# A fused decoder layer: whole projection tiles on TensorE, the step size inside the decay exponent, and a copy moved from VectorE to ScalarE

## The chip, the cores and the metric

The kernel runs on one core of one Trainium2 chip. The metric is the device time of one launch in microseconds, as the median of several runs. One launch computes a whole decoder layer, for 4 sequences of 256 tokens with 256 channels each (1024 tokens).

## The reference, cut to what matters

The layer has three parts, each followed by a residual sum and a layer norm: a state-space mixer with 32 heads, an expert layer chosen by token id, and a mixture of 16 experts with two picks per token. The change touches only the mixer:

```
proj = x @ Win.T                          # per head: x (64), z (64), B (128), C (128), and dt
dt   = softplus(dt_raw + dt_bias)
xc, Bc, Cc = silu(causal_conv(x)), silu(causal_conv(B)), silu(causal_conv(C))   # 4 taps in time
decay = exp(dt * A);  dtx = dt * xc
h_t = decay_t * h_(t-1) + dtx_t outer B_t;  y_t = h_t . C_t
y = y * rsqrt(mean(y*y) + 1e-6) * silu(z);  out = y @ Wout.T
```

The kernel does not step through time. With the running sum cum of dt * A inside a sequence, y_t is the sum over s <= t of (C_t . B_s) * exp(cum_t - cum_s) * dt_s * xc_s. That is a score matrix from B and C, weighed by a decay matrix, and then multiplied by x.

## The kernel before, in words

**Tiling.** The 32 heads are taken in 16 pairs (NPAIR). The projection of a pair has 6 tiles of 128 channels (NTILE): tile 0 is x of both heads, tiles 1 to 4 are B and C of head 0 and head 1, tile 5 is z. Each tile is computed for 1024 tokens in two halves of 512; one half (`project(j)`, tile j // 2, half j % 2) fills one PSUM bank with 6 matmuls of 512 columns, a product of split float32 numbers in three terms over two blocks of 128 input channels. The halves use PSUM banks 0 to 3 in turn (`ps[:, j % 4, :]`), so a tile may start only when the tile two before it has been read out. `half_read` gives the semaphore for that.

**Software pipeline.** `steps` runs steps 0 to 17. Step n does the projection and convolution of pair n (front), the scores and half of the mixing of pair n-1 (mid), and the rest of the mixing and the norm of pair n-2 (tail). Step 0 has only the front, step 1 front and mid, steps 2 to 15 all three, step 16 mid and tail, step 17 the tail. Every engine has its own written-out order of work within a step; each executes in that order, and semaphores tie them together.

**TensorE (line 529 on).** In a step: project(0); mix(2) and mix(3) and mean_square(0) of the tail; x_to_tokens(0); project(1); x_to_tokens(1); project(2); project(3); score(0); and from then on one score after each half, with mean_square(1) after the score of j = 4 and mix(0), mix(1) after the one of j = 8. `x_to_tokens(c)` turns four 128x128 blocks of the convolved x into bank 4 + c. `score(k)` (batch k // 2, head k % 2) writes bank 4 + k % 2. It waits for two things: the silu of B and C, and `ge(pe, S["v_m"], q * UNITS + k - 1)` at line 564, that is, for VectorE's weigh(k-2), which read the same bank (for k < 2 it waits for `x_scaled`, `v_xs`, instead). `mix(p, b)` multiplies x by the weighed scores and waits for weigh(2b+1).

**ScalarE (line 857 on).** z(0) and z(1) of the pair before at the start of a step. Then `copy(j)` for j = 0 to 9, one per projected half: it reads the PSUM bank, multiplies by the last tap and writes conv. Between these copies stand, at fixed places (`work`), the silu of tile 4, the table loads, squares, exp_decay(b) (the exponential of two decay matrices), and rsqrt (a logarithm and an exponential). The four other silus close the step.

**VectorE (line 1077 on).** For each tile m the taps of the convolution add shifted multiples out of PSUM. `tap(m, i)` with s = 1 waits for the copies of the halves it covers (`S["a_copy"]`). The table `TAPS_OF` (line 33) gives 6 half-wide taps for tile 0 and 4 for the others: s = 1 whole, s = 2 whole, s = 3 on each half. The s = 3 taps release the PSUM banks. At fixed places (`between`) stand `x_scaled` (line 1080: the turned x times dt into xs), `weigh(k)` (line 1089: score times decay, in place) and `gate` (y times silu(z)).

**GpSimd (line 335 on).** Splits the next pair's weights, builds the decay exponents (`log_decay`: cum_t minus cum_s, plus a causal mask), subtracts low parts (`low_part`), and multiplies the norm in (`norm`). SyncE loads a pair's weights and cum rows two steps ahead.

The lines on which the order hangs:

```
                    if mid and 3 <= j < 3 + UNITS:
                        score(j - 3)
...
                    for k, at_ in enumerate(((1, 0), (2, 0), (2, 1), (3, 0), (3, 1), (4, 0), (4, 1), (4, 3))):
                        between[at_] = [lambda k=k: weigh(k)]
```

The second says: weigh(k) stands just before tap number i of tile m, for at_ = (m, i).

Of the kernel before, what the change touches and what calls it, by code (L numbers as in the profile page):

```python
# [19 lines left out]
P = 128  # L20
# [12 lines left out]
TAPS_OF = [[(slice(h, h + 1), s) for h in (0, 1) for s in (1, 2, 3)] if m == 0 else  # L33
           [(slice(0, 2), 1), (slice(0, 2), 2), (slice(0, 1), 3), (slice(1, 2), 3)] for m in range(NCONV)]
# [20 lines left out]
HIT = 3.0e38  # L55
LN_EPS = 1e-5
# [3 lines left out]
def build_layer(nc, xT, x, winT, wdtT, a_log, dt_bias, woutT, ids, ctxT, gateT, ebias, wsh, wgu, wdn, out):  # L60
# [4 lines left out]
    with ExitStack() as ctx:  # L65
# [17 lines left out]
        dt_tok = sb("dt_tok", [P, TB, H])  # L83
# [60 lines left out]
        def take(n):  # L144
# [32 lines left out]
                 "a_copy a_z a_silu a_decay a_sq a_ln a_rs "  # L177
                 "v_tap v_xs v_m v_yz v_y "
# [52 lines left out]
        def _(sp):  # L231
# [15 lines left out]
            sp.wait_ge(S["d_dt"], 3)  # L247
# [18 lines left out]
            sp.wait_ge(S["v_xs"], 2 * NPAIR)  # L266
# [42 lines left out]
        def _(pool):  # L309
# [65 lines left out]
            def step(n, par, split_next, mid, tail, ahead):  # L375

                if mid:
                    log_decay(n - 1, 1 - par, 2)
                if tail:
                    low_part(n - 2, 1)  # L380
                if mid:
                    log_decay(n - 1, 1 - par, 3)
                if split_next:
                    split(n + 1, 1 - par)
                if tail:
                    norm(n - 2, par, 0)
                    norm(n - 2, par, 1)
                if mid:
                    low_part(n - 1, 0)
                if ahead:  # L390
                    log_decay(n, par, 0)
                    log_decay(n, par, 1)
# [102 lines left out]
        def _(pe):  # L495
# [9 lines left out]
            def turn_dt():  # L505

                pe.wait_ge(S["d_dt"], 3)
                pe.wait_ge(S["z_const"], 10)
                for i, src in enumerate((dt_l, dt_cum)):
                    for b in range(TB):  # L510
                        mm = pe.transpose(ps[:, 4 + i, b * H:(b + 1) * H], src[:, b * P:(b + 1) * P],
                                          ident[0:H, 0:H])
                mm.then_inc(S["s_dtT"], 1)
                pe.wait_ge(S["d_dtT"], 1)
# [14 lines left out]
            def step(n, par, front, mid, tail):  # L529
# [26 lines left out]
                def score(k):  # L556
                    b, h = k // 2, k % 2
                    c0, c1 = cols[b]
                    Bm, Cm = conv[:, qp, 1 + 2 * h, :], conv[:, qp, 2 + 2 * h, :]
                    ge(pe, S["a_silu"], q * NCONV + 3 + 2 * h)  # L560
                    if k < 2:
                        ge(pe, S["v_xs"], q * 2 + k + 1)
                    else:
                        ge(pe, S["v_m"], q * UNITS + k - 1)
                    pe.matmul(ps[:, 4 + k % 2, 0:T], Bm[:, c0:c0 + P], Cm[:, c0:c0 + T], start=True, stop=True)  # L565
                    pe.matmul(ps[:, 4 + k % 2, T:SC], Bm[:, c1:c1 + P], Cm[:, c1:c1 + P], start=True, stop=True  # L566
                              ).then_inc(S["s_done"], 1)

                def mix(p, b):

                    g = b // 2
                    ge(pe, S["v_m"], p * UNITS + 2 * b + 2)
                    if b % 2 == 0:
                        ge(pe, S["v_xs"], p * 2 + 1 + g)
                        ge(pe, S["a_ln"], p * 2 - 1 + g)
                    for j, (c, t) in enumerate(((0, T), (T, SC))):
                        for h in range(2):
                            ch = slice(h * HP, (h + 1) * HP)
                            mm = pe.matmul(ps[ch, 6 + g, (b % 2) * T + j * P:(b % 2) * T + T], xs[:, 2 * b + j, ch],  # L579
                                           decay[:, 2 * b + h, c:t], start=(j == 0), stop=(j == 1),  # L580
                                           skip_group_check=True)
                            if j == 1:
                                mm.then_inc(S["y_done"], 1)
# [12 lines left out]
                for j in range(2 * NTILE):  # L596
                    if front:
                        project(j)
                    if tail and j == 0:
# [6 lines left out]
                    if mid and j < 2:  # L606
                        x_to_tokens(j)
                    if mid and 3 <= j < 3 + UNITS:
                        score(j - 3)
                    if mid and j == 8:  # L610
                        mix(q, 0)
                        mix(q, 1)
                    if tail and j == 4:
                        mean_square(r, 1)
# [218 lines left out]
        def _(act):  # L833
# [22 lines left out]

            def step(n, par, front, mid, tail):
# [13 lines left out]
                def copy(j):  # L871
                    tile, hf = j // 2, j % 2
                    ge(act, S["u_done"], n * 12 + j + 1)
                    if j == 0 and not (isinstance(n, int) and n < 2):
# [3 lines left out]
                                   scale=w_raw[:, par, tap:tap + 1]).then_inc(S["a_copy"], 1)  # L878

# [25 lines left out]
                if isinstance(n, int) and n == 0:  # L905
                    work[0] += [lambda: softplus(0)]
                    work[1] += [lambda: softplus(1), lambda: softplus(2)]
                    work[2] += [lambda: softplus(3)]
                if mid:
                    work[0] += [lambda: silu(q, qp, 4)]  # L910
                if tail:
                    work[1] += [lambda: square(r, 1)]
                if mid or tail:
                    work[1] += [lambda: act.preload_act_table_set("natural_log_exp_and_others")]
                if mid:
                    for b, j in enumerate((2, 4, 6, 8)):
                        work[j] += [lambda b=b: exp_decay(b)]
                    work[8].append(lambda: square(q, 0))
                if tail:
                    work[3] += [lambda: rsqrt(r, 0)]  # L920
                    work[6] += [lambda: rsqrt(r, 1)]
# [122 lines left out]
        def _(dve):  # L1044
# [8 lines left out]
            def sum_dt():  # L1053
# [9 lines left out]
                link(dve.tensor_tensor(dt_l, dt_l, dt_ch, ALU.add))  # L1063
                link(dve.tensor_scalar(dt_da, dt_l, head_c[:, 2:3], -1.0, ALU.mult, ALU.mult))
# [4 lines left out]

            def take_dt():  # L1070
                dve.wait_ge(S["s_dtT"], 1)
                dve.tensor_copy(dt_tok[:, :, :], ps[:, 4, 0:TB * H].rearrange("p (b h) -> p b h", b=TB))
                dve.tensor_copy(cum_tok[:, :, :], ps[:, 5, 0:TB * H].rearrange("p (b h) -> p b h", b=TB)  # L1073
# [3 lines left out]
            def step(n, par, front, mid, tail):  # L1077
                q, qp, r, rp = n - 1, 1 - par, n - 2, par

                def x_scaled(c):  # L1080

                    ge(dve, S["xt_done"], q * 2 + c + 1)
                    ge(dve, S["y_done"], q * UNITS)
                    dve.tensor_tensor(xs[:, 4 * c:4 * c + 4, :].rearrange("p b (h c) -> p b h c", h=2),  # L1084
                                      ps[:, 4 + c, :].rearrange("p (b h c) -> p b h c", b=4, h=2),
                                      dt_tok[:, 4 * c:4 * c + 4, bass.ds(q * 2, 2)].unsqueeze(3)
                                      .broadcast_to([P, 4, 2, HP]), ALU.mult).then_inc(S["v_xs"], 1)
# [34 lines left out]
                if mid:  # L1122
                    between[0, 3] = [lambda: x_scaled(0)]
                    between[0, 5] = [lambda: x_scaled(1)]
                    for k, at_ in enumerate(((1, 0), (2, 0), (2, 1), (3, 0), (3, 1), (4, 0), (4, 1), (4, 3))):
                        between[at_] = [lambda k=k: weigh(k)]
                    between[4, 2] = [lambda: gate(q, qp, 0)]
                if tail:
                    between[0, 4] = [lambda: gate(r, rp, 1)]
                if isinstance(n, int) and n == 0:  # L1130
                    between[1, 0] = [sum_dt]
                for m in range(NCONV):
                    for i in range(len(TAPS_OF[m])):
                        for f in between.get((m, i), []):
                            f()
                        if front:
                            tap(m, i)
            steps(dve, step, take_dt)
# [253 lines left out]
```

## Time and profile before

| | us |
|---|---|
| median of 3 runs (lowest, highest) | 762.57 (761.0, 764.87) |
| the profiled execution, its own time | 762.01 |
| its span, first to last instruction | 760.3 |
| TensorE busy (share of the span) | 676.9 (89%) |
| VectorE busy | 522.8 (69%) |
| ScalarE busy | 430.1 (57%) |
| GpSimd busy | 437.8 (58%) |

The mixer's steps take the first two thirds of the span; the expert parts follow and are the same in both kernels. Durations of matmuls overlap: one starts before the end of the last is recorded, so the distance between starts (the pitch) tells what one costs. The same holds on the other engines by some 0.1 us: an instruction's pitch is a little under its duration where the next one does not depend on it. In the listings, PE is TensorE, PEld its weight load, DVE VectorE, ACT ScalarE, POOL GpSimd, and Lnnn the line of the kernel.

### The profile page before, as it was taken

To read this page: it belongs to the slowest core of one execution; us is meant where nothing else is said; L and a number is where in the kernel's file an instruction comes from. 1 tells how busy PE (TensorE), PEld (TensorE's weight loads), DVE (VectorE), ACT (ScalarE), POOL (GpSimd) and SP (SyncE) were. 2 spreads that over 40 slices of the span, in tenths; PEclk is the share of its full clock that TensorE was granted. 3 is DMA by queue.
4 is the path that set the end of the run, shared out by engine and by line. 5 is a ranking of instruction groups with operands and counts; after the bars stand their busy time and mean duration, and the time that the engine had idled before them with its cause. 6 is when DMAs were issued, how large, how long until landed. Compare 5 with 4: busy or idle time off the path is not lost.

```text
span 760.3 us, 11331 instructions
## 1 busy us (share of the span) xinstructions
PE 676.9 (89%) x3376; PEld 521.3 (69%) x3376; DVE 522.8 (69%) x803; ACT 430.1 (57%) x701; POOL 437.8 (58%) x382
## 2 busy tenths in 40 slices
PE   6599999999999999999999999899999986999930
PEld 3477777777777777777777777688846864677720
DVE  5988988988989989989889889512337343222236
ACT  4366777787787687687777777721011242333321
POOL 4076887787787777878868864754000014733134
PEclk9899999999999999999999999999999998999975
DMA  3221121121111211211211200430092401333324
GB/s 141 117 87 54 56 98 42 55 86 50 57 51 61 81 42 57 95 42 55 97 42 55 97 0 0 141 110 1 1 339 75 111 21 28 93 99 99 79 72 128
DMA packets 19968, 57.41 MB, mean 76 GB/s; under 512 B 2998, under 2 KB 13110, under 8 KB 17206
## 3 DMA queue, kind: packets, MB, share of 16 engines
q1 hardware_dynamic: 17686, 50.92, 19.6%
q0 software_dynamic: 2256, 6.16, 3.3%
q8 instruction: 14, 0.23, 0.1%
q14 instruction: 12, 0.10, 0.0%
HBM read 50.78 MB, written 6.29 MB: 75 GB/s over the span
## 4 chain that ended last, share of the span: by engine, by line
PE 51%; DVE 23%; issue 12%; ACT 9%; POOL 2%; DMA 1%; DVEq 1%; ACTq 0%; SPq 0%; POOLq 0%
DVE conv L1109 18%; PE ps L551 13%; PE ps L524 7%; PE ps L579 6%; PE ps L745 5%; PE ps L671 4%; PE ps L645 4%; PE ps L785 4%; ACT conv L877 3%; DVE decay L1093 2%; POOL conv L489 2%; ACT decay L883 2%; ACT y_hi L888 1%; PE ps L763 1%; PE ps L565 1%
## 5 line engine op out<-in xcount | busy, mean ns | idle before, releaser
L1109 DVE SCALAR_TENSOR_TENSOR conv<-ps,w_raw,conv 128x506 f32<-128x506 f32 (+3 forms) x352 | 324.6, 935 | 48.2 <-ACT conv L877 44.6
L551 PE MATMUL ps<-x_hi,w_hi 128*128 128x512 f32 x384 | 166.1, 433 | 29.8 <-DVE conv L1109 27.2
L877 ACT ACTIVATE conv<-ps,w_raw 128x512 f32<-128x512 f32 x160 | 109.3, 684 | 109.4 <-PE ps L551 109.2
L551 PE MATMUL ps<-x_hi,w_lo 128*128 128x512 f32 x384 | 151.6, 395 | 0.0
L551 PE MATMUL ps<-x_lo,w_hi 128*128 128x512 f32 x384 | 151.1, 393 | 0.0
L353 POOL TENSOR_TENSOR decay<-cum_b,cum_tok 128x512 f32<-128x512 f32 (+1 forms) x128 | 103.3, 829 | 35.5 <-DVE cum_tok L1073 23.8
L551 PEld LDWEIGHTS ps<-x_hi,w_hi 128*128 128x128 f32 x384 | 72.7, 189 | 56.2 <-DVE conv L1109 41.7
L373 POOL TENSOR_TENSOR y_lo<-y_sq,y_hi 128x512 fp32r<-128x512 f32 x32 | 41.3, 1289 | 80.1 <-ACT y_sq L889 80.1
L359 POOL TENSOR_TENSOR decay<-decay,mask 128x512 f32<-128x512 f32 x64 | 82.7, 1292 | 5.0
L551 PEld LDWEIGHTS ps<-x_hi,w_lo 128*128 128x128 f32 x384 | 72.5, 189 | 16.8
L551 PEld LDWEIGHTS ps<-x_lo,w_hi 128*128 128x128 f32 x384 | 73.0, 190 | 10.1
L862 ACT ACTIVATE conv<-conv 128x1024 f32<-128x1024 f32 x80 | 79.4, 1049 | 0.2
L565 PE MATMUL ps<-conv 128*128 128x256 f32 x256 | 76.4, 380 | 2.0 <-DVE xs L1084 1.6
L1093 DVE TENSOR_TENSOR decay<-ps,decay 128x384 f32<-128x384 f32 x128 | 70.2, 549 | 7.4 <-ACT decay L883 4.9
L937 ACT ACTIVATE ln_v<-ln_m,eps_ln 128x1 f32<-128x1 f32 x24 | 7.1, 295 | 90.6 <-DVE ln_m L1159 90.6
L524 PE MATMUL ps<-late,y_all 128*128 128x256 f32 x256 | 56.7, 379 | 0.2 <-DVE xs L1148 0.2
L565 PEld LDWEIGHTS ps<-conv 128*128 128x128 f32 x256 | 47.5, 188 | 13.2 <-issue 2.5
L458 POOL DMA_INDIRECT xb<-x_scratch,y_all x31 | 30.0, 967 | 42.5 <-PE ps L721 37.5
L343 POOL TENSOR_TENSOR w_lo<-w_raw,w_hi 128x1536 fp32r<-128x1536 f32 x15 | 53.0, 3531 | 1.2
L883 ACT ACTIVATE decay<-decay 128x768 f32<-128x768 f32 x64 | 53.4, 836 | 0.0
L566 PEld LDWEIGHTS ps<-conv 128*128 128x128 f32 x256 | 48.5, 190 | 6.7
L524 PEld LDWEIGHTS ps<-late,y_all 128*128 128x128 f32 x256 | 48.2, 190 | 6.9 <-DVE xs L1148 0.6
(166 smaller groups left out, 1027.1 us busy)
## 6 DMA issues: line engine op xcount, KB each, us to landing
cum_b<-cum_scratch SPq DMA_DIRECT2D x16, 1024.0 KB, 4.7
w_raw<-in_winT SPq DMA_DIRECT2D x16, 778.0 KB, 4.4
y_all<-in_wgu SPq DMA_DIRECT2D x4, 1408.0 KB, 10.7
ys_scratch<-y_blk SPq DMA_DIRECT2D x31, 128.0 KB, 1.7
late<-in_wdn SPq DMA_DIRECT2D x2, 1408.0 KB
late<-in_woutT SPq DMA_DIRECT2D x1, 2048.0 KB, 8.2
y_all<-in_xT SPq DMA_DIRECT2D x1, 1024.0 KB, 4.9
conv<-in_x SPq DMA_DIRECT2D x1, 1024.0 KB, 5.5
```

Source lines behind the costliest of these rows:

```text
L343: pool.tensor_tensor(w_lo[:, par, :], raw, w_hi[:, par, :].bitcast(F32), ALU.subtract).then_inc(S["w_split"], 1)
L353: pool.tensor_tensor(decay[:, 2 * b:2 * b + 2, c:t], cum_b[:, qp, :, b * T + j * P:(b + 1) * T], cum_tok[:, 2 * b + j, bass.ds(q * 2, 2)]. ...
L359: pool.tensor_tensor(diag, diag, mask[:, :].unsqueeze(1).unsqueeze(1).broadcast_to([P, 2, 2, P]), ALU.add).then_inc(S["p_arg"], 1)
L524: mm = pe.matmul(ps[:, b % 2, 0:D], y_all[:, i, b * P:(b + 1) * P], wo_sb[:, i, :], start=(i == 0), stop=(i == NPAIR - 1))
L551: mm = pe.matmul(ps[:, j % 4, :], wp[:, par, w], xp[:, kk, t], start=(i == 0), stop=(i == 5))
L565: pe.matmul(ps[:, 4 + k % 2, 0:T], Bm[:, c0:c0 + P], Cm[:, c0:c0 + T], start=True, stop=True)
L566: pe.matmul(ps[:, 4 + k % 2, T:SC], Bm[:, c1:c1 + P], Cm[:, c1:c1 + P], start=True, stop=True).then_inc(S["s_done"], 1)
L862: act.activation(conv[:, pp, tile, :], conv[:, pp, tile, :], ACT.Silu).then_inc(S["a_silu"], 1)
L877: act.activation(conv[:, par, tile, hf * 512:(hf + 1) * 512], ps[:, j % 4, :], ACT.Copy, scale=w_raw[:, par, tap:tap + 1]).then_inc(S["a_c ...
L883: act.activation(d, d, ACT.Exp).then_inc(S["a_decay"], 1)
L1093: dve.tensor_tensor(decay[:, k, :], ps[:, 4 + k % 2, 0:SC], decay[:, k, :], ALU.mult).then_inc(S["v_m"], 1)
L1109: dve.scalar_tensor_tensor(out=o[:, :, s:], in0=u[:, :, 0:T - s], scalar=w_raw[:, par, c:c + 1], in1=o[:, :, s:], op0=ALU.mult, op1=ALU.ad ...
```

## The change

On TensorE the two halves of a tile are projected back to back, and everything else stands between tiles: after tile 0 the tail's mixes and mean square and both x_to_tokens, after tiles 1 to 4 two scores each (before the last two of these mix(0), mix(1)). On VectorE x_scaled is gone, tile 0 has 4 taps like the others, and the weighs and gates stand at other places. On ScalarE the turned x is copied by `take_x`, and squares and rsqrt stand at other places. dt_s is no longer multiplied into x: instead cum_s - log(dt_s) takes the place of cum_s in the decay exponent. The dt part in step 0 gains a lower clamp of dt, a logarithm and a subtraction, and the turning of dt into tokens falls away.

```diff
-TAPS_OF = [[(slice(h, h + 1), s) for h in (0, 1) for s in (1, 2, 3)] if m == 0 else
-           [(slice(0, 2), 1), (slice(0, 2), 2), (slice(0, 1), 3), (slice(1, 2), 3)] for m in range(NCONV)]
+TAPS_OF = [[(slice(0, 2), 1), (slice(0, 2), 2), (slice(0, 1), 3), (slice(1, 2), 3)] for m in range(NCONV)]
...
 GpSimd, step():
                     log_decay(n - 1, 1 - par, 2)
+                    log_decay(n - 1, 1 - par, 3)
                 if tail:
                     low_part(n - 2, 1)
-                if mid:
-                    log_decay(n - 1, 1 - par, 3)
...
 TensorE, turn_dt():
-                pe.wait_ge(S["d_dt"], 3)
+                pe.wait_ge(S["d_dt"], 5)
...
-                for i, src in enumerate((dt_l, dt_cum)):
-                    for b in range(TB):
-                        mm = pe.transpose(ps[:, 4 + i, b * H:(b + 1) * H], src[:, b * P:(b + 1) * P],
-                                          ident[0:H, 0:H])
+                for b in range(TB):
+                    mm = pe.transpose(ps[:, 4, b * H:(b + 1) * H], dt_ch[:, b * P:(b + 1) * P], ident[0:H, 0:H])
...
 TensorE, score(k):
                     if k < 2:
-                        ge(pe, S["v_xs"], q * 2 + k + 1)
+                        ge(pe, S["a_xs"], q * 2 + k + 1)
...
 TensorE, step():
-                for j in range(2 * NTILE):
+                for tile in range(NTILE):
                     if front:
-                        project(j)
-                    if tail and j == 0:
+                        project(2 * tile)
+                        project(2 * tile + 1)
+                    if tail and tile == 0:
                         mix(r, 2)
                         mix(r, 3)
                         mean_square(r, 0)
...
-                    if mid and j < 2:
-                        x_to_tokens(j)
-                    if mid and 3 <= j < 3 + UNITS:
-                        score(j - 3)
-                    if mid and j == 8:
+                    if mid and tile == 0:
+                        x_to_tokens(0)
+                        x_to_tokens(1)
+                    if mid and tile == 4:
                         mix(q, 0)
                         mix(q, 1)
-                    if tail and j == 4:
+                    if mid and 1 <= tile < 5:
+                        score(2 * tile - 2)
+                        score(2 * tile - 1)
+                    if tail and tile == 2:
                         mean_square(r, 1)
...
 ScalarE:
+            def log_dt():
+                act.wait_ge(S["d_dt"], 2)
+                act.activation(dt_ch, dt_e, ACT.Ln).then_inc(S["a_dt"], 1)
...
+                def take_x(c):
+                    ge(act, S["xt_done"], q * 2 + c + 1)
+                    ge(act, S["y_done"], q * UNITS)
+                    act.activation(xs[:, 4 * c:4 * c + 4, :], ps[:, 4 + c, :].rearrange("p (b c) -> p b c", b=4), ACT.Copy
+                                   ).then_inc(S["a_xs"], 1)
...
+                    work[4] += [log_dt]
                 if mid:
                     work[0] += [lambda: silu(q, qp, 4)]
-                if tail:
-                    work[1] += [lambda: square(r, 1)]
                 if mid or tail:
                     work[1] += [lambda: act.preload_act_table_set("natural_log_exp_and_others")]
                 if mid:
+                    work[2] += [lambda: take_x(0), lambda: take_x(1)]
+                if tail:
+                    work[3] += [lambda: square(r, 1), lambda: rsqrt(r, 0)]
+                if mid:
                     for b, j in enumerate((2, 4, 6, 8)):
                         work[j] += [lambda b=b: exp_decay(b)]
-                    work[8].append(lambda: square(q, 0))
+                    work[9].append(lambda: square(q, 0))
                 if tail:
-                    work[3] += [lambda: rsqrt(r, 0)]
-                    work[6] += [lambda: rsqrt(r, 1)]
+                    work[7] += [lambda: rsqrt(r, 1)]
...
 VectorE:
                 link(dve.tensor_tensor(dt_l, dt_l, dt_ch, ALU.add))
+                link(dve.tensor_scalar(dt_e, dt_l, DT_MIN, None, ALU.max))
...
+            def less_log_dt():
+                dve.wait_ge(S["a_dt"], 6)
+                dve.tensor_tensor(dt_ch, dt_cum, dt_ch, ALU.subtract).then_inc(S["d_dt"], 1)
...
-                dve.tensor_copy(dt_tok[:, :, :], ps[:, 4, 0:TB * H].rearrange("p (b h) -> p b h", b=TB))
...
-                def x_scaled(c):
...
-                    between[0, 3] = [lambda: x_scaled(0)]
-                    between[0, 5] = [lambda: x_scaled(1)]
-                    for k, at_ in enumerate(((1, 0), (2, 0), (2, 1), (3, 0), (3, 1), (4, 0), (4, 1), (4, 3))):
+                    for k, at_ in enumerate(((2, 0), (2, 1), (3, 0), (3, 1), (4, 0), (4, 1))):
                         between[at_] = [lambda k=k: weigh(k)]
-                    between[4, 2] = [lambda: gate(q, qp, 0)]
+                    between[4, 3] = [lambda: weigh(6)]
                 if tail:
-                    between[0, 4] = [lambda: gate(r, rp, 1)]
+                    between[1, 2] = [lambda: gate(r, rp, 1)]
                 if isinstance(n, int) and n == 0:
                     between[1, 0] = [sum_dt]
+                    between[3, 0] = [less_log_dt]
...
+                if mid:
+                    weigh(7)
+                    gate(q, qp, 0)
```

## Rows read from the trace of the kernel before

**Rows 1.** The profile page: TensorE's busy time, and its granted clock in 40 slices.
```profile
PE 676.9 (89%) x3376; PEld 521.3 (69%) x3376; DVE 522.8 (69%) x803; ACT 430.1 (57%) x701; POOL 437.8 (58%) x382
...
PEclk9899999999999999999999999999999998999975
```

**Rows 2.** Waits, 73 to 477 us: engine, line, releaser: total us, times, longest.
```profile
PEld ps L551 <- DVE conv L1109: 29.6, 41, 1.4
```

**Rows 3.** ScalarE in order: start us, us, engine, line, operation; in brackets idle before.
```profile
211.51 3.90 ACT L862 ACTIVATE conv<-conv 128x1024 f32<-128x1024 f32 x4
215.32 1.06 ACT L868 ACTIVATE z_gate<-ps 128x512 f32<-128x512 f32 x2
...
220.10 0.69 ACT L877 ACTIVATE conv<-ps,w_raw 128x512 f32<-128x512 f32 x1 [2.20 <-PE ps L551]
220.69 0.60 ACT L888 ACTIVATE y_hi<-ps 128x512 fp32r<-128x512 f32 x1
...
221.78 1.28 ACT L914 ACT_TABLE_LOAD   x1
...
223.67 0.84 ACT L883 ACTIVATE decay<-decay 128x768 f32<-128x768 f32 x1
...
224.97 0.69 ACT L894 ACTIVATE y_all<-ps,eps_rms 128x512 f32<-128x512 f32 x1
...
250.91 1.28 ACT L914 ACT_TABLE_LOAD   x1
```

**Rows 4.** TensorE's matmuls in order, in the same step; first start and count.
```profile
216.05 1.52 PE L579 MATMUL ps<-decay,xs 128*64 128x256 f32 x16
217.50 0.50 PE L588 MATMUL ps<-y_hi,mean_w 128*128 128x512 f32 x1
...
218.43 0.48 PE L551 MATMUL ps<-x_hi,w_hi 128*128 128x512 f32 x1
...
219.90 0.60 PE L536 MATMUL ps<-ident,conv 128*128 128x128 f32 x4
...
220.26 0.48 PE L551 MATMUL ps<-x_hi,w_hi 128*128 128x512 f32 x1
...
223.10 0.59 PE L565 MATMUL ps<-conv 128*128 128x256 f32 x2
...
223.68 0.47 PE L551 MATMUL ps<-x_hi,w_hi 128*128 128x512 f32 x1
...
243.62 0.50 PE L551 MATMUL ps<-x_hi,w_hi 128*128 128x512 f32 x1 [0.91 <-DVE conv L1109]
```

**Rows 5.** VectorE in order, in the same step.
```profile
220.83 0.75 DVE L1109 SCALAR_TENSOR_TENSOR conv<-ps,w_raw,conv 128x510 f32<-128x510 f32 x1 [0.93 <-ACT conv L877]
...
234.25 1.27 DVE L1109 SCALAR_TENSOR_TENSOR conv<-ps,w_raw,conv 128x1020 f32<-128x1020 f32 x1
235.44 0.55 DVE L1093 TENSOR_TENSOR decay<-ps,decay 128x384 f32<-128x384 f32 x1
235.90 2.70 DVE L1109 SCALAR_TENSOR_TENSOR conv<-ps,w_raw,conv 128x1016 f32<-128x1016 f32 x3
238.52 0.55 DVE L1093 TENSOR_TENSOR decay<-ps,decay 128x384 f32<-128x384 f32 x1
```

**Rows 6.** Groups by line, all of the span: busy us, mean ns; idle before.
```profile
L1117 DVE TENSOR_TENSOR z_gate<-ps,z_gate 128x512 f32<-128x512 f32 x32 | 22.0, 687 | 6.8 <-ACT y_sq L889 6.8
```

**Rows 7.** TensorE in step 16: the first matmuls of a score after a wait.
```profile
482.13 0.67 PE L565 MATMUL ps<-conv 128*128 128x256 f32 x2 [1.17 <-DVE xs L1084]
```

**Rows 8.** VectorE in step 0: two operations on the dt arrays.
```profile
19.74 1.21 DVE L1063 TENSOR_TENSOR y_all<-y_all 32x1024 f32<-32x1024 f32 x1 [0.63 <-ACT y_all L855]
20.99 0.74 DVE L1064 TENSOR_SCALAR y_all<-y_all,head_c 32x1024 f32<-32x1024 f32 x1
```

**Rows 9.** TensorE in step 0: the first matmul after its longest wait there.
```profile
27.65 0.79 PE L551 MATMUL ps<-x_hi,w_hi 128*128 128x512 f32 x1 [6.84 <-DVE conv L1109]
```

**Rows 10.** Two microseconds of step 0: length, then each engine's busy time (instructions), PEclk, DMA.
```profile
28.00:30.00 2.00, 2.00 (x6) 1.52 (x6) 1.96 (x3) 0.00 (x0) 0.00 (x0) 0.50 1.03 430
```

More of the change, by code:

```diff
@@ L55 @@
 HIT = 3.0e38
+DT_MIN = 1.0e-30
 LN_EPS = 1e-5
@@ L82, in build_layer @@
         cum_b = sb("cum_b", [P, 2, 2, NT])
-        dt_tok = sb("dt_tok", [P, TB, H])
         cum_tok = sb("cum_tok", [P, TB, H])
@@ L176, in build_layer @@
                  "w_split u_done p_arg p_lo s_done xt_done y_done ms_done "
-                 "a_copy a_z a_silu a_decay a_sq a_ln a_rs "
-                 "v_tap v_xs v_m v_yz v_y "
+                 "a_copy a_z a_silu a_xs a_decay a_sq a_ln a_rs "
+                 "v_tap v_m v_yz v_y "
                  "ld_wo ld_xt ld_late ld_rt ln_st "
@@ L246, in _ @@
             load_pair(1, 1)
-            sp.wait_ge(S["d_dt"], 3)
+            sp.wait_ge(S["d_dt"], 4)
             sp.dma_start(cum_dram, dt_cum).then_inc(S["st_cum"], 16)
@@ L265, in _ @@
             sp.wait_ge(S["s_done"], NPAIR * UNITS)
-            sp.wait_ge(S["v_xs"], 2 * NPAIR)
+            sp.wait_ge(S["a_xs"], 2 * NPAIR)
             sp.wait_ge(S["xt_done"], 2 * NPAIR)
@@ L573, in mix @@
                     if b % 2 == 0:
-                        ge(pe, S["v_xs"], p * 2 + 1 + g)
+                        ge(pe, S["a_xs"], p * 2 + 1 + g)
                         ge(pe, S["a_ln"], p * 2 - 1 + g)
@@ L1068, in sum_dt @@
                 link(ins)
+            def less_log_dt():
+                dve.wait_ge(S["a_dt"], 6)
+                dve.tensor_tensor(dt_ch, dt_cum, dt_ch, ALU.subtract).then_inc(S["d_dt"], 1)
             def take_dt():
                 dve.wait_ge(S["s_dtT"], 1)
-                dve.tensor_copy(dt_tok[:, :, :], ps[:, 4, 0:TB * H].rearrange("p (b h) -> p b h", b=TB))
-                dve.tensor_copy(cum_tok[:, :, :], ps[:, 5, 0:TB * H].rearrange("p (b h) -> p b h", b=TB)
+                dve.tensor_copy(cum_tok[:, :, :], ps[:, 4, 0:TB * H].rearrange("p (b h) -> p b h", b=TB)
                                 ).then_inc(S["d_dtT"], 1)
@@ L1078, in step @@
                 q, qp, r, rp = n - 1, 1 - par, n - 2, par
-                def x_scaled(c):
[L1082 to L1087, printed above, removed]
                 def weigh(k):
```

## The prediction

> **What bounds the kernel now.** I read the page first: TensorE is busy 89% of the span at nearly full clock [rows 1]. Then the waits of the steady steps 2 to 15: the projection's weight loads waited 29.6 us for VectorE's taps, at most 1.4 us at a time [rows 2], some 2.1 us in each of 14 steps. Last the engines' orders in one step. One full step takes 250.91 - 221.78 = 29.13 us, from one table load to the same one a step later [rows 3].
>
> Prices by start to start. TensorE [rows 4]: a tile of two halves back to back 2.84 (220.26 to 223.10), a lone half 1.47 (218.43 to 219.90), a score 0.58, a pair of mixes 1.45, x_to_tokens 0.36, mean square and x_to_tokens together 0.93, so the mean square 0.57. A step now: 12 x 1.47 + 8 x 0.58 + 2 x 1.55 (0.1 for the change of kind) + 2 x 0.57 + 2 x 0.36 = 27.2, and with some 2 of waits it is the 29.1. So TensorE bounds it, held up by VectorE through the PSUM banks of the projection. In the new order the sum is 6 x 2.84 + the same = 26.6; without a single wait 2.5 us could be had per step.
>
> **Lags.** A copy starts 0.20 after TensorE has gone on from the half (219.90, 220.10), and the tap 0.73 after the copy [rows 3, 4, 5]: 0.93 together. VectorE: tap s = 1 to the weigh behind it 1.19, weigh 0.46, s = 2 with both s = 3 taps 2.62 [rows 5], so 1.30, 0.66, 0.66. A weigh ends 0.55 after its start, and its waiter starts 0.05 later. The gate is 0.69 long [rows 6], 0.60 by pitch as a weigh of 0.55 has 0.46. ScalarE [rows 3]: copy 0.59, exp_decay and copy 1.30, so exp_decay 0.71, the two squares 1.09, table load 1.28, four silus 3.8, z(0) and z(1) 1.0, a logarithm or an exponential of rsqrt 0.6 to 0.7.
>
> **The part that decides: where scores wait.** score(k) waits for weigh(k-2), before and after. Before, score(3) came after the first half of tile 3, and weigh(1) before the taps of tile 2: always ready. Now score(3) comes right after tile 2, and weigh(1) stands behind tap(2,0), which needs both copies of that same tile 2. TensorE must stand still meanwhile, and tile 3 stands behind score(3) on it. The same for score(5) with weigh(3) and tap(3,0), and for score(7) with weigh(5) and tap(4,0). From the end of a tile on TensorE: 0.93 + 1.19 + 0.60 = 2.72 until the odd score may start. The even score covers 0.58; two mixes and a score (2.13) cover most in the case of score(7). What is queued behind: mean_square(1), tile 3, tile 4, tile 5, and through them the copies, that is, everything.
>
> **A full step in the new order,** tile 0 starting at 0:
> - Tile 0 to 2.84, mixes to 4.38, mean square and two x_to_tokens to 5.66, tile 1 to 8.50. Its banks wait for z(0), z(1): ScalarE finishes its silus at 1.8 and z at 2.8, in time. Then copy 0, silu of tile 4, and copy 1 at 4.2; the taps of tile 0 run from 4.9 to 8.9.
> - ScalarE takes copy 2 at 7.33, take_x(0) at 7.92, take_x(1) at 8.51, exp_decay(0) at 9.10, copy 3 at 9.81. take_x is no row of before. Nearest are the copy out of PSUM of equal size (0.59 by pitch, 0.69 long) and z (0.53 by pitch); I take the copy's 0.59, bounds 0.5 to 0.7. score(0) waits 0.14 for it; scores 0 and 1 end at 9.8. Tile 2 runs to 12.64.
> - VectorE starts tile 1 at 10.54, 1.1 later than tile 1's end allows, because two take_x and exp_decay(0) stand before copy 3. Two taps, gate(1), two taps: weigh(0) at 14.96, score(2) at 15.56. TensorE has waited since 12.64: 2.9 us. tap(2,0) at 15.42 (its copies are there at 14.8, behind squares, logarithm, exponential and exp_decay(1)), weigh(1) at 16.61, score(3) at 17.21: another 1.1.
> - A score after a wait takes longer, 0.67 for its first two matmuls against 0.59 [rows 7, 4]; I take 0.67 for it. Mean square: tile 3 starts at 18.46, ends 21.30. score(5) at 24.02 (wait 2.14), tile 4 24.69 to 27.53. Mixes, score(6) to 29.65, score(7) at 30.25 (wait 0.6), tile 5 30.92 to 33.76.
>
> VectorE ends tile 4, weigh(7) and gate(0) 7 us after tile 4's end, before the next step's mix(3) and mean square want them. GpSimd, in its new order: log_decay(2), log_decay(3), then low_part(1), ready near 13, wanted at 18; the split of weights ends near 19, wanted at the next step. So these edits cost nothing, hidden by TensorE's longer step. SyncE's loads are two steps ahead and only get more time.
>
> So 33.76 against 29.13: **+4.6 per full step,** 14 x 4.62 = +64.7. Removed from VectorE are two x_scaled (0.6 each) and the extra starts of tile 0's six half taps; from TensorE 0.6 of interrupted tiles. They are in the sum and buy nothing, as the chain runs through tap, weigh, score.
>
> **Ends.** Leaving step 15, before had no 0.91 stall of the next tile 0 [rows 4]; the new step has none to save: +0.9. Step 1 has no gate and no squares before copy 4; with VectorE about 1.0 less late, +3.6. Step 16: take_x behind silu and table load, scores in pairs: +0.8 (an estimate, bounds -0.5 and +2). Step 0: VectorE gains the clamp, 0.74, and the subtraction, 1.21, both on its path to turn_dt [rows 8], loses about 0.6 of taps and 0.3 of a copy, but starts when both halves of tile 0 are copied: +1.0, bounds 0 and 2. ScalarE's extra logarithm there lies in idle time. The experts are untouched. Sum +71.0 on the profiled execution's 762.0 (its span 760.3 and 1.7 around it; the median of the runs is 762.6): **833 us**.
>
> **A rule against the change, weighed.** Row: after a wait of 6.84 us in step 0 the clock was 0.50 of full, that is 1.2 and not 2.4 GHz, and six matmuls started in 2 us [rows 9, 10]; in the steps, with waits up to 1.4, the tenths stay at 9 [rows 1, 2]. My longest wait is 2.9. By the rows it could go either way, nearer to the short waits. The Trainium skill, "TensorE: Matmul & The Clock Gate", section "A second HAM failure mode: psum-queue depth-cycling", says that frequent short idle times between groups of matmuls that cycle through PSUM banks can make the clock fall and rise again and again. No run here shows it; by that rule the time is that of rival B, without it the sum above.
>
> **Rivals.**
> - A, VectorE is not late: score(2) never waits and only the chain tile, copy, tap, weigh, odd score is left. score(3) then starts 2.72 after tile 2's end, at 15.36 instead of 17.21: 31.9 per step, +2.8, x 14 = +39, with ends +5: 806. For it: my 1.1 of ScalarE delay rests on take_x, unseen. Against: even then tile 1's taps and gate fill the time.
> - B, the clock falls once per step in the 2.9 wait. Some eight matmuls at 0.43 instead of 0.24 cost 1.6: +22, 855. Against: tile 3 and what follows keep TensorE at work.
> - C, faster: weigh(1), weigh(3) and weigh(5) are done when their odd scores come, and TensorE runs through. Then 26.8 per step, -2.3 x 14, with +1 at the start: 731. It decides at the end of tile 2: weigh(1) must have ended within 0.5 us of it. For it: VectorE has 1.8 us less to do per step. Against: weigh(1) is ordered behind a tap of that very tile, so by the code no speed of VectorE can do it.
> - D, nothing: waits and savings cancel, as in a chain of only one late score (33.76 would have to be 29.1): 762.
>
> **Chances.** Forecast 0.78 (its own range 820 to 846, from take_x, the extra per late score, and the ends), A 0.08, B 0.08, C 0.04, D 0.02. The range from 805 to 857 takes in A and B, since both are the same mechanism at other sizes. A change of under 0.5%, some 4 us, can't be told from none in this kernel. Faster 0.04, same 0.02, slower 0.94.
>
> **What would show it.** TensorE's wait of scores for the weighs (L565 for L1093, or their shifted lines), 0 in the steps now, at some 6.5 us per step; the projection's wait for taps near 0. Table loads 33.8 apart. VectorE's waits for copies up from tiles 0 and 4 to all tiles but 2. Copy 3 right behind exp_decay(0). Wrong would be: scores that never wait (C), no wait before score(2) (A), a granted clock under 0.9 in the steps (B), or the projection still waiting for taps.

## The result and the profile after

The changed kernel takes 857.1 us (median of 4 runs, 854.6 to 859.0) against 763.7 for the kernel before: a ratio of 1.123, 95% interval 1.118 to 1.127. The forecast was 833, with a range of 805 to 857. The direction and most of the size were right; the time lies at the far end of the range, outside by 0.1 us.

The page of the changed kernel, TensorE's busy time and the granted clock in 40 slices, beside [rows 1]:

```profile
PE 712.3 (83%) x3368; PEld 542.6 (63%) x3368; DVE 499.0 (58%) x740; ACT 443.5 (52%) x734; POOL 436.9 (51%) x382
...
PEclk9899998999989999999999999898999999999985
```

Two things are to be read there. VectorE, which held TensorE up before, works 24 us less (522.8 to 499.0) and the kernel is slower all the same: its work was no longer what bounds it. And TensorE is busy 35 us longer with 8 instructions fewer: some of its matmuls run slower.

The waits of the changed kernel from 80 to 570 us (engine, line, releaser: us in total, times, longest), beside [rows 2]:

```profile
DVE conv L1117 <- ACT conv L881: 152.7, 56, 4.7
...
PEld ps L561 <- DVE decay L1101: 87.6, 56, 2.8
...
PE ps L561 <- DVE decay L1101: 73.3, 56, 2.4
```

L561 is the first matmul of a score and L1101 is weigh. The 29.6 us that the projection waited for taps [rows 2] have given way to 73 us in which scores wait for weighs: 56 times, four in each of 14 steps. VectorE now waits 152.7 us for the copies of each tile. The two engines take turns where they had overlapped.

TensorE in one full step of the changed kernel, beside [rows 4] (start, us, first form of the group; in brackets idle before):

```profile
288.81 0.39 PE L547 MATMUL ps<-x_hi,w_hi 128*128 128x512 f32 x1
...
294.43 0.47 PE L547 MATMUL ps<-x_hi,w_hi 128*128 128x512 f32 x1
...
304.11 0.70 PE L561 MATMUL ps<-conv 128*128 128x256 f32 x2 [2.41 <-DVE decay L1101]
...
305.76 1.22 PE L561 MATMUL ps<-conv 128*128 128x256 f32 x2 [0.73 <-DVE decay L1101]
...
308.06 0.63 PE L547 MATMUL ps<-x_hi,w_hi 128*128 128x512 f32 x1
...
313.86 0.70 PE L561 MATMUL ps<-conv 128*128 128x256 f32 x2 [1.91 <-DVE decay L1101]
...
320.07 0.70 PE L561 MATMUL ps<-conv 128*128 128x256 f32 x2 [0.26 <-DVE decay L1101]
```

VectorE in the same step, beside [rows 5]:

```profile
299.10 1.28 DVE L1117 SCALAR_TENSOR_TENSOR conv<-ps,w_raw,conv 128x1020 f32<-128x1020 f32 x1 [1.41 <-ACT conv L881]
...
303.51 0.55 DVE L1101 TENSOR_TENSOR decay<-ps,decay 128x384 f32<-128x384 f32 x1
303.97 1.27 DVE L1117 SCALAR_TENSOR_TENSOR conv<-ps,w_raw,conv 128x1020 f32<-128x1020 f32 x1
305.16 0.55 DVE L1101 TENSOR_TENSOR decay<-ps,decay 128x384 f32<-128x384 f32 x1
```

Tile 0 starts at 288.81 and tile 1 at 294.43, 5.62 us later (forecast 5.66). score(2) starts 15.3 us behind tile 0's start (forecast 15.56), behind the weigh of 303.51; score(3) 16.95 us behind it (forecast 17.21), behind the weigh of 305.16, which stands behind the tap of tile 2 at 303.97. From here the step is slower than forecast: the score at 305.76 takes 1.22 us for its first two matmuls and not 0.67, and the matmuls behind it 0.63 instead of 0.39. The granted clock of another step shows why (length, busy time of PE, PEld, DVE, ACT, POOL, then PEclk, DMA share, GB/s):

```profile
230.00:232.00 2.00, 0.61 (x3) 0.18 (x1) 2.00 (x4) 2.00 (x4) 2.00 (x2) 1.00 0.81 332
232.00:234.00 2.00, 0.98 (x4) 0.73 (x4) 2.00 (x3) 0.07 (x1) 1.92 (x2) 0.91 0.00 0
234.00:236.00 2.00, 1.42 (x6) 1.15 (x5) 1.97 (x4) 0.00 (x0) 2.00 (x1) 0.50 0.00 0
236.00:238.00 2.00, 2.00 (x7) 1.61 (x7) 1.70 (x3) 0.00 (x0) 1.79 (x2) 0.50 0.00 0
238.00:240.00 2.00, 2.00 (x7) 1.52 (x6) 0.00 (x0) 0.23 (x1) 0.00 (x0) 0.50 0.00 0
```

TensorE stands still from 230.6 to 233.0 us, and the clock falls to half, 1.2 GHz, at 233.6, in the middle of the next matmuls. Between 200 and 440 us this happens once in each of the seven steps, five times for 3.4 us and twice for 6.8 us, and in the kernel before not once in that stretch. A full step takes 35.28 us on average ((540.06 - 81.48) / 13, by its table loads, L923), where 33.76 was forecast and 29.13 it was [rows 3]. The 13 steps fall into two groups: nine with 3.4 us at half clock take 34.8 to 35.1 us, four with 6.8 us of it 36.1 to 36.2.

### The profile page after: what moved, and what is told of

Same layout as the page of the kernel before. It is cut to its first block, busy times and chain, and to the rows that moved or that the text cites. A ratio compares the mean times of both kernels' runs of the same rounds, so it can differ in the third digit from the quotient of the medians.

```text
span 857.3 us, 11229 instructions
## 1 busy us (share of the span) xinstructions
PE 712.3 (83%) x3368; PEld 542.6 (63%) x3368; DVE 499.0 (58%) x740; ACT 443.5 (52%) x734; POOL 436.9 (51%) x382
## 4 chain that ended last, share of the span: by engine, by line
PE 58%; DVE 15%; issue 12%; ACT 10%; POOL 2%; DMA 1%; DVEq 0%; ACTq 0%; SPq 0%; POOLq 0%
PE ps L547 20%; DVE conv L1117 8%; PE ps L520 6%; PE ps L561 5%; PE ps L744 4%; ACT conv L881 4%; DVE decay L1101 4%; PE ps L670 3%; PE ps L644 3%; PE ps L784 3%; PE ps L575 3%; ACT decay L893 2%; PE ps L562 2%; POOL conv L487 2%; PE ps L532 2%
## 5 line engine op out<-in xcount | busy, mean ns | idle before, releaser
L1117 DVE SCALAR_TENSOR_TENSOR conv<-ps,w_raw,conv 128x1020 f32<-128x1020 f32 (+1 forms) x320 | 316.7, 1007 | 169.8 <-ACT conv L881 166.2
L561 PE MATMUL ps<-conv 128*128 128x256 f32 x256 | 92.5, 445 | 82.8 <-DVE decay L1101 80.3
L547 PE MATMUL ps<-x_lo,w_hi 128*128 128x512 f32 x384 | 156.8, 408 | 0.0
L547 PE MATMUL ps<-x_hi,w_lo 128*128 128x512 f32 x384 | 155.5, 405 | 0.0
L561 PEld LDWEIGHTS ps<-conv 128*128 128x128 f32 x256 | 42.3, 201 | 108.5 <-DVE decay L1101 87.6
L547 PEld LDWEIGHTS ps<-x_hi,w_hi 128*128 128x128 f32 x384 | 77.8, 203 | 28.1 <-DVE conv L1117 10.3
L547 PEld LDWEIGHTS ps<-x_hi,w_lo 128*128 128x128 f32 x384 | 76.7, 200 | 18.0
L547 PEld LDWEIGHTS ps<-x_lo,w_hi 128*128 128x128 f32 x384 | 77.5, 202 | 15.2
L367 POOL TENSOR_TENSOR y_all<-z_gate,y_all 128x512 f32 (+1 forms) x32 | 40.9, 1279 | 82.4 <-ACT y_all L906 82.4
L1101 DVE TENSOR_TENSOR decay<-ps,decay 128x384 f32<-128x384 f32 x128 | 70.2, 549 | 5.6 <-PE ps L562 5.4
L562 PE MATMUL ps<-conv 128*128 128x128 f32 x256 | 54.4, 298 | 0.0
```

What stands on the lines that cost most here:

```text
L547: mm = pe.matmul(ps[:, j % 4, :], wp[:, par, w], xp[:, kk, t], start=(i == 0), stop=(i == 5))
L1101: dve.tensor_tensor(decay[:, k, :], ps[:, 4 + k % 2, 0:SC], decay[:, k, :], ALU.mult).then_inc(S["v_m"], 1)
L1117: dve.scalar_tensor_tensor(out=o[:, :, s:], in0=u[:, :, 0:T - s], scalar=w_raw[:, par, c:c + 1], in1=o[:, :, s:], op0=ALU.mult, op1=ALU.ad ...
```

## The experiments

Theory: (1) the odd score behind a whole tile waits for a weigh that stands behind a tap of the same tile; (2) VectorE starts tile 1 late as ScalarE has the copies of x ahead of copy(3); (3) what the sum lacks is the clock. Rivals: whole tiles as such or the copy on ScalarE cost the time; or the missing 1.5 us per step are a wait and not the clock.

| label | edit | us | ratio to before (95%) |
|---|---|---|---|
| (the change) | | 857.1 | 1.123 (1.118 to 1.127) |
| e1_pairs | weighs in pairs | 793.0 | 1.037 (1.034 to 1.041) |
| e2_filler | filler in one wait | 841.2 | 1.101 (1.097 to 1.104) |
| e3_takex_early | take_x ahead of copy(2) | 839.9 | 1.100 (1.096 to 1.104) |
| e4_old_order | old order, rest kept | 772.4 | 1.011 (1.008 to 1.015) |
| e5_x_on_dve | x copy on VectorE | 845.9 | 1.107 (1.103 to 1.111) |
| e6_pairs_early | e1 and e3 | 788.7 | 1.032 (1.029 to 1.036) |
| e7_pairs_early_gate | e6, gate later | 773.4 | 1.012 (1.010 to 1.015) |
| e8_old_takex_late | e4, take_x(1) later | 765.6 | 1.002 (1.000 to 1.005) |
| e9_lag | whole tiles, scores one tile later | 740.8 | 0.970 (0.968 to 0.973) |
| e10_filler_all | filler in all long waits | 831.1 | 1.088 (1.085 to 1.092) |

**e1_pairs: the odd weighs ahead of the tap.**

```diff
-                    for k, at_ in enumerate(((2, 0), (2, 1), (3, 0), (3, 1), (4, 0), (4, 1))):
-                        between[at_] = [lambda k=k: weigh(k)]
+                    for m in (2, 3, 4):
+                        between[m, 0] = [lambda k=2 * m - 4: weigh(k), lambda k=2 * m - 3: weigh(k)]
```

> The changed kernel with one edit: on VectorE weigh(1), weigh(3), weigh(5) stand right behind weigh(0), weigh(2), weigh(4), ahead of the s = 1 tap of the tile and not behind it. Theory (the odd score waits for a tap of the tile that TensorE has just finished): the waits before score(3), score(5), score(7) vanish, the one before score(2) stays at some 2.4 us. A full step, by the same sum as in the prediction, takes 30.1 us if the clock then stays up, 31.7 if it still falls once; changed kernel 35.3. Time 784 us, or 807 with the fall. Rival (whole tiles as such, or the copy on ScalarE, cost the time): the time stays over 840 us.

793.0 us, between the two figures. One edit of the order on VectorE, with the same instructions, gives back 64 of the 93 us. Its waits from 80 to 480 us:

```profile
PEld ps L561 <- DVE decay L1101: 41.9, 32, 2.8
PE ps L561 <- DVE decay L1101: 31.1, 13, 2.4
```

One wait of 2.4 us is left per step, the one before score(2). The clock falls in every second step only; its table loads at 384.37, 415.74 and 445.79 us give a step of 31.4 with a fall and one of 30.05 without, where 31.7 and 30.1 were expected. The rival is refuted. Not all of the 64 us is the order's own: at full clock a step of the change takes 33.4 us (e10 below) and one here 30.05, which is 47 us over 14 steps. The other 17 us or so come from the clock, which falls in seven of the 14 steps for 3.4 us, where the change has it in all 14, with 6.8 us of half clock in five of them.

**e2_filler and e10_filler_all: more work, less time.** The filler's result goes to bank 6 after its last reader and is overwritten unread.

```diff
+                    if front and tail and tile == 2:
+                        ge(pe, S["a_ln"], r * 2 + 1)
+                        for i in range(8):
+                            pe.matmul(ps[:, 6, :], w_hi[:, par, 0:P], x_hi[:, 0, 0:512], start=True, stop=True)
                     if mid and 1 <= tile < 5:
                         score(2 * tile - 2)
```

> The changed kernel with eight more 512-column matmuls (their result is overwritten unread) between tile 2 and score(2) in steps 2 to 15, in the 2.4 us that TensorE waits there. More work, no wait shorter. Theory (the idle time at scores 2 and 3 lets the clock fall to 1.2 GHz for some 4 to 6 us of each step): the granted clock of the steps goes from some 0.93 to 1.00, a full step from 35.3 to 33.7 us, the time from 857 to 835 us. Rival (the extra 1.5 us per step are not the clock's but a wait that I missed): 857 us or, since the filler takes 1.9 of 2.4 us and may delay the score, up to 862.

841.2 us: 16 us faster, and 6 us short of what was expected. The clock still fell, now in every second step (at 237, 305 and 373.5 us of the stretch 200 to 440). Between two table loads a step with a fall takes 35.0 us and one without 33.4: the same instructions in one trace, 1.6 us apart. So the second run filled the others as well: 9 matmuls before score(2), 3 between scores 2 and 3, 7 between scores 4 and 5.

> The changed kernel with more 512-column matmuls in steps 2 to 15 whose result is overwritten unread, in all its long waits: 9 ahead of score(2), 3 between score(2) and score(3), 7 between score(4) and score(5). The first filler, 8 in the first wait alone, had the clock fall in every second step still. Theory (idle time of TensorE in these waits, and not one wait alone, decides on the clock; the sum of the prediction at full clock holds): no half microsecond of the steps under full clock, a full step of 33.4 to 33.8 us, time 833 us. Rival (the clock falls for another reason, or fillers delay the scores as much as they save): 841 us or more.

831.1 us. The stretch from 80 to 480 us, first of the filled kernel, then 80 to 570 us of the changed one:

```profile
80.00:480.00 400.00, 388.91 (x2003) 300.40 (x2002) 289.85 (x360) 275.41 (x396) 272.89 (x217) 1.00 0.15 56
```

```profile
80.00:570.00 490.00, 416.71 (x2053) 322.97 (x2050) 337.11 (x417) 317.39 (x456) 307.75 (x246) 0.93 0.14 48
```

266 matmuls more (14 steps of 19) and 26 us less; a step takes 351.62 - 318.27 = 33.35 us. The scores still start where VectorE lets them, as the sum has it. In this step tile 1, score(2) and score(3) start at

```profile
319.03 0.47 PE L547 MATMUL ps<-x_hi,w_hi 128*128 128x512 f32 x1
...
328.72 0.70 PE L561 MATMUL ps<-conv 128*128 128x256 f32 x2 [0.35 <-DVE decay L1110]
...
330.37 0.70 PE L561 MATMUL ps<-conv 128*128 128x256 f32 x2
```

and score(2) comes 9.69 us and score(3) 11.34 us behind tile 1's start, where the sum had 9.90 and 11.55. So what the filler takes away is the slow clock, and that cost 26 us. The time is within 2 us of the prediction's sum, 833 us. A part of that is luck: the 14 steps are 0.37 us shorter than in the sum, 5 us together, and about 3 us are lost again outside them (in step 1, which has no filler, the clock was at half for 10.2 us of the profiled execution).

**e3_takex_early: ScalarE's part.** `work[2] += take_x(0), take_x(1)` becomes `work[1] += ...`, behind the table load.

> The changed kernel with both take_x on ScalarE ahead of copy(2), after the table load, where ScalarE idles, and not behind copy(2). Theory (VectorE starts tile 1 late by 1.1 us since the copies of x stand before copy(3)): copy(3) and score(2) come 1.1 us earlier per step, time 857 - 15 = 842 us; if the shorter wait also keeps the clock up, 1.5 us more per step, 820 us. Rival (VectorE isn't late through ScalarE): 857 us, within 3.

839.9 us, 2 us from the first figure, and VectorE was late through ScalarE. The first tap of tile 1,

```profile
255.10 2.59 DVE L1117 SCALAR_TENSOR_TENSOR conv<-ps,w_raw,conv 128x1020 f32<-128x1020 f32 x2 [0.49 <-ACT conv L881]
```

starts 0.92 us after tile 1's end on TensorE, where it was 1.84 us in the changed kernel. So the delay was 0.9 us and not 1.1. The wait before score(2) fell from 2.4 to 1.7, and the clock still fell once in every step, but for 3.4 us and never for 6.8. That is a second part of the gain, and the nearness to the first figure, which held the clock's share fixed, is partly luck. A step takes 34.1 us, 0.8 less than the 34.9 of the changed kernel's steps with as short a fall: 11 us over 14 steps. The other 6 us are mostly the falls that became shorter.

**e5_x_on_dve: the copy back on VectorE.** `take_x` moves as it is to VectorE (`tensor_copy`), to `between[1, 0]`.

> The changed kernel with the two copies of the turned x on VectorE again (plain copies, right behind the taps of tile 0), and none on ScalarE. Theory: VectorE then has them in the 1.4 us in which it waits for copy(3), and starts tile 1 some 0.4 us earlier than in the changed kernel: 857 - 6 = 851 us. Rival (the copy on ScalarE is a cost of its own of 1.1 us per step, as the run with an earlier take_x could suggest): 842 us or less. No change in the three other waits per step.

845.9 us, between the two. VectorE had idle time before tile 1 (1.41 us in the row at 299.10 above), so the copy cost little there, and ScalarE could hand over copy(3) earlier. The table loads tell the two parts of the 11 us apart. The clock stayed up in four of the 14 steps, and these take 33.07 us; at full clock the changed kernel's step takes 33.4 (e10). That is 0.3 us per step, 4 us in all, near the 0.4 that was expected. The rest, some 7 us, is the clock, which fell in ten steps for 3.4 us each. One wait is new and was not expected: score(0) now waits 1.0 us for the copy on VectorE, and the wait before score(2) is 1.1 us and not 2.4. Moving work off VectorE did not help here.

**e4_old_order and e8_old_takex_late: the change without its order.** The halves, taps, scores, squares, gates and GpSimd's order are those of the kernel before; what stays is the copy of x on ScalarE and dt in the exponent. In e8 `take_x(1)` goes from `work[2]` to `work[3]`.

> The changed kernel with the old order everywhere: single halves with one score after each, six taps for tile 0, squares, gates and weighs at their old places; what is left of the change is the dt in the exponent and the copy of the turned x on ScalarE (take_x(0) ahead of copy(1), take_x(1) behind copy(2)). Theory (the order alone made the loss): 762 to 772 us, since take_x(1) delays exp_decay(0) and copy(3) by 0.6 us per step while VectorE's saving of 1.2 us lies before a wait. Rival (the copy on ScalarE or the dt exponent carries part of the loss): over 785 us.

> The kernel with the old order, dt in the exponent and the copy on ScalarE, but take_x(1) behind copy(3) and not behind copy(2). Theory (its 9 us over the kernel before are weigh(0) waiting for an exp_decay(0) that take_x(1) delays by 0.6 us): weigh(0) no longer waits more than 0.3 us, score(1) waits some 0.5 us for take_x(1), which the 0.9 us stall before the next tile 0 takes in: 762 us. Rival (the dt exponent or the prologue costs the 9 us): 771.

772.4 and 765.6 us (1.0025, interval 1.0003 to 1.0046). So the order made all of the loss but 2 to 9 us. The waits of e4 and then e8, 80 to 480 us, show where the 9 came from:

```profile
DVE decay L1100 <- ACT decay L892: 16.7, 14, 1.2
```

```profile
DVE decay L1100 <- ACT decay L892: 9.2, 13, 0.7
...
PE ps L563 <- ACT xs L886: 5.7, 14, 0.4
```

weigh(0) waited up to 1.2 us for an exponential behind take_x(1). Putting that copy one place later brought 7 of the 9 us; a wait of 0.7 stayed where 0.3 was expected. The dt exponent is free within 3 us, and the 1.2 us of VectorE that are saved per step buy nothing in the old order: a full step of e8 takes 29.13 us, as in the kernel before.

**e6_pairs_early and e7_pairs_early_gate: the parts together.** e6 is e1 and e3; e7 also moves gate(1) from `between[1, 2]` to behind weigh(1) in `between[2, 0]`.

> The changed kernel with both edits: weighs in pairs ahead of each tile's taps, and both take_x ahead of copy(2). Theory: VectorE starts tile 1 1.1 us earlier, the one wait left, before score(2), is 1.3 us, and the clock stays up: a full step of 29.3 to 29.5 us, time 768 us. If the clock still falls, 785. Rival (the gain of the earlier take_x is lost because the taps bound the step once the odd scores are free): 790.

> As the run before it, and gate(1) on VectorE moved from the middle of tile 1 to behind weigh(1). weigh(0) and score(2) come another 0.6 us earlier; VectorE then works without a pause from tile 1 to tile 4, 19 us, and its only idle time is at tile 0. A full step of 28.9 us, clock at 1.00: 760 us, that is, level with the kernel before. If VectorE's chain from tile 1 on is what bounds it, the move saves nothing of it: 768.

788.7 and 773.4 us. Both missed: e6 by 20 us against the first figure, close to the one with a fall. Its longest wait was 2.0 us and not 1.3. The two take_x, now behind the table load, end 0.3 us too late for copy(2), so VectorE starts tile 1 0.64 us earlier than in e1 (1.20 us after tile 1's end against 1.84) and not 1.1; and tile 2 itself ends 0.2 us earlier, which makes the wait longer again. The clock fell in 13 of the 14 steps. The one without a fall takes 106.95 - 77.54 = 29.41 us, inside the 29.3 to 29.5 expected for the clock up; the others take 30.7. In e7 the longest wait was 1.5 us:

```profile
110.00:450.00 340.00, 313.71 (x1690) 247.72 (x1689) 282.80 (x348) 262.13 (x379) 262.93 (x205) 1.00 0.17 63
```

The clock is at 1.00 in its steps, and that is all of the 15 us between the two: a step of e7 takes 29.55 us, no less than e6's one step at full clock. Moving the gate shortened the wait before score(2), but not the step, as the expectation's second case had it (VectorE's chain from tile 1 on bounds the step); the 28.9 us of the first case were 0.65 us too few. VectorE sits idle for 4.5 us before tile 0, since copy(1) stands on ScalarE behind four silus, z and one more silu.

**e9_lag: whole tiles with a tile of slack.** With e7's weighs and gate, and on TensorE:

```diff
-                    if tail and tile == 0:
+                    if tail and tile == 1:
                         mix(r, 2)
                         mix(r, 3)
                         mean_square(r, 0)
...
-                    if mid and tile == 0:
+                    if mid and tile == 1:
                         x_to_tokens(0)
                         x_to_tokens(1)
...
-                    if mid and 1 <= tile < 5:
-                        score(2 * tile - 2)
-                        score(2 * tile - 1)
+                    if mid and tile >= 2:
+                        score(2 * tile - 4)
+                        score(2 * tile - 3)
```

and mean_square(1) and mix(0), mix(1) behind the scores of tiles 3 and 4. On ScalarE the silu of tile 4 stands behind copy(1), then the table load, and exp_decay(0), square(1), take_x(0), take_x(1) behind copy(3); the other exp_decays and both rsqrt move to later copies too.

> Whole tiles kept, but everything else one tile later: on TensorE tiles 0 and 1 back to back, then mixes, mean square and x_to_tokens; scores 0 and 1 behind tile 2, 2 and 3 behind tile 3, 4 and 5 behind tile 4 (then mix(0), mix(1)), 6 and 7 behind tile 5. Weighs in pairs ahead of tiles 2, 3, 4, gate(1) behind weigh(1); ScalarE's order fitted: copies 0 and 1 first, then silu and table load, take_x behind copy(3). Theory (whole tiles are good where each score's weigh has a tile's time of slack, and VectorE can go from tile 0 into tile 1 without a pause): no wait of a score for a weigh over 0.3 us, a full step of 27 to 28 us against 29.1 of the kernel before, clock at 1.00, time 735 to 750 us. Rival (the z tile and ScalarE's 23 us of work hold the step where it was): 760 us or more.

740.8 us: 3.0% faster than the kernel before (2.7 to 3.2%). VectorE in one step, and TensorE's waits from 80 to 480 us:

```profile
320.42 7.96 DVE L1123 SCALAR_TENSOR_TENSOR conv<-ps,w_raw,conv 128x1020 f32<-128x1020 f32 x8 [2.48 <-ACT conv L881]
328.30 1.15 DVE L1107 TENSOR_TENSOR decay<-ps,decay 128x384 f32<-128x384 f32 x2
```

```profile
PEld ps L547 <- DVE conv L1123: 6.4, 18, 0.4
```

VectorE goes from tile 0 into tile 1 without a pause (eight taps in one group) and waits for copies once per step, 2.5 us instead of four times. In the full steps no score waits for a weigh. A step takes 348.62 - 321.35 = 27.3 us, near the 26.6 us that the prediction gave for TensorE's own work without a wait.

## Why the prediction was right and where it failed

**Where scores wait: right.** The rule that weigh(1), weigh(3) and weigh(5) are ordered behind a tap of the very tile just projected was read from the code, and its 2.72 us from rows of before. e1 takes away this alone and gives back 64 us, 47 of them at equal clock. The projection no longer waits for taps in the steps, and VectorE waits for copies at all tiles but 2, both as forecast.

**The schedule of the step: right to 0.4 us.** score(2) at 15.3 against 15.56, score(3) at 16.95 against 17.21; waits of 2.4, 0.7, 1.9 and 0.3 us against 2.9, 1.1, 2.1 and 0.6 (the trace counts less idle time, as it draws the matmul before them to its end). With the clock held up, 33.4 us per step against 33.76 and 831 us against 833. The copy on ScalarE takes 0.48 by pitch, below my 0.5 to 0.7; that is why VectorE is late by 0.9 us and not 1.1.

**Savings that buy nothing: right.** VectorE has 24 us less to do and waits instead (e8: the same saving in the old order, no gain).

**The clock: wrong, and this is the step that failed.** The forecast priced it at nothing, since its longest wait of 2.9 us lay nearer to waits that had not moved the clock (1.4) than to the one that had (6.84) [rows 2, 9], and gave rival B 0.08. It falls in every step and costs 26 us (e10): 833 and 26 are 859, and 857.1 was measured. B's price for one fall was right: 1.6 us, where e2 shows 1.6 and the changed kernel 34.9 - 33.4 = 1.5. B's 22 us fell short since five of the 14 steps have 6.8 us at half clock and not 3.4, and cost some 2.7 us each. B's sign, a clock under 0.9 in the steps, was set too low: 0.93 went with a fall in every step.

The yardstick, the longest wait, was wrong too, and the trace of before could have told it, in the experts' part, which the forecast did not look at. TensorE's last two waits before 615 us and the next long one, then the granted clock (length, busy times, PEclk third from the end):

```profile
612.11 0.41 PE L626 MATMUL ps<-ident,conv 128*128 128x128 f32 x2 [0.99 <-issue]
612.76 0.44 PE L626 MATMUL ps<-ident,conv 128*128 128x128 f32 x2 [0.24 <-DVE conv L1165]
...
630.04 0.94 PE L708 MATMUL ps<-y_all,conv 128*128 128x62 bf16 x12 [3.75 <-POOL y_all L473]
```

```profile
612.00:615.00 3.00, 2.65 (x19) 2.23 (x20) 0.91 (x6) 2.62 (x7) 0.00 (x0) 0.99 0.25 87
615.00:618.00 3.00, 3.00 (x7) 1.73 (x6) 2.20 (x25) 0.84 (x3) 0.57 (x1) 0.50 0.00 0
...
628.00:630.00 2.00, 0.00 (x0) 0.00 (x0) 2.00 (x2) 0.00 (x0) 1.99 (x2) 0.65 0.04 8
```

The clock fell at 615.0 us, with no wait over 1.0 us in the 48 us before, and again at 628.6, inside a wait of 3.75 us. The second is the 8 near the end of the clock's line in [rows 1]. So a fall needs no wait as long as 2.9 us, and B should have had far more than 0.08, and the range room behind B's price. How often the clock would fall in the new steps these rows could not tell.

The Trainium skill, "TensorE: Matmul & The Clock Gate", "A second HAM failure mode: psum-queue depth-cycling", describes falls from short idle times between groups of matmuls. By that rule, the trace agrees in the changed kernel (0.93 in the steps); but it gives no size, and the waits of up to 1.4 us in the kernel before and of 1.5 and 0.7 us in every step of e7 came without a fall in the steps.

**Rival A** (VectorE not late): refuted. The changed kernel has the wait before score(2), and e3 takes away 0.9 us of VectorE's delay and gains by it. **C:** not so in the changed kernel, but e1 and e9 show that it needed only another order.

## What to carry to other kernels

When two engines pass work back and forth, look up for each wait what stands before its releaser in that engine's order: if it is an operation on data that the waiting engine has only just made, the two take turns, and a saving elsewhere on either does not help. Put the consumer a whole tile later. And a few idle times of 2 us in every loop turn can cost TensorE's clock as well: where waits are that long, price the slow clock in.

## What the runs showed of the hardware

- The clock fell in kernels whose longest wait per step was 2.4 (the change, every step), 2.4 (e1, every second step), 2.0 (e6, 13 of 14 steps) and 1.9 us (e3, every step; e5, ten of 14; e2, every second one), and did not at 1.5 us (e7) or with the waits filled (e10). The length of the longest wait does not order them: e1 has a longer one than e6 and falls half as often. Nor does their sum: e7 waits 2.2 us per step and never falls, e6 2.0 us. And in the experts' part of the kernel before it fell with no wait over 1.0 us in 48 us. What decides stays open.
- A fall lasted 3.4 us, in some steps of the changed kernel 6.8 us, with TensorE back at work for most of it. One of 3.4 us costs 1.3 us of a step in e1 (31.4 against 30.05) and e6 (30.7 against 29.4), 1.6 us in e2 (35.0 against 33.4) and e5 (34.7 against 33.1). In the changed kernel all falls together cost 26 us, 1.9 us per step.
- Nineteen matmuls per step whose results nobody reads made the kernel 26 us faster.
